# Layer-1 convolution stage: the outputs' inverse scale on GpSimd, hidden tiles transposed one step later

## The reference, cut to what matters

```python
def act_quant(x):
    scale = 127.0 / jnp.clip(jnp.max(jnp.abs(x), axis=-1, keepdims=True), 1e-05)
    return jnp.clip(jnp.round(x * scale), -128, 127) / scale

h = bit_linear(x, w1)                       # layernormed x, quantised; ternary weights; 256 -> 1024
h = depthwise_conv1d(h.transpose(0, 2, 1), conv_w, conv_b)   # three taps along the tokens
h = jax.nn.silu(h.transpose(0, 2, 1))
x = x + bit_linear(h, w2)                   # h quantised by its own maximum per token; 1024 -> 256
```

## Time and profile before

| what | value |
|---|---|
| median of three runs | 3378.53 us |
| the profiled execution's own time | 3373.19 us |
| its span | 3371.5 us |
| busy over the span: TensorE, VectorE, ScalarE, GpSimd | 92%, 73%, 52%, 39% |
| 3079.24 to 3318.11 us: busy of 238.87 us, TensorE | 205.34 us |
| the same, VectorE | 223.69 us |
| the same, ScalarE | 222.33 us |
| the same, GpSimd | 202.39 us |

### The profile page before, as it was taken

One profiled execution on the slowest core, in us unless ns is written; L12 is line 12 of the kernel. 1 busy time (PEld: TensorE's weight loads), 2 busy tenths in 40 slices (PEclk: granted clock), 3 DMA queues, 4 the chain that ended last, 5 costly groups with the idle time before them and its releaser, 6 DMA issues. The chain is left out here.

```text
span 3371.5 us, 63871 instructions
## 1 busy us (share of the span) xinstructions
PE 3090.4 (92%) x23118; PEld 2677.0 (79%) x23118; DVE 2453.9 (73%) x5435; ACT 1760.1 (52%) x4520; POOL 1303.3 (39%) x1199
## 2 busy tenths in 40 slices
PE   6999999999999999999999899999999973168887
PEld 5888888888888888888888788888888861046665
DVE  6666666666666666666666787878787849889998
ACT  5565656565656565656564323232323325169997
POOL 2333333333333333333332333343434320058886
PEclk9999999999999999999999999999999985589999
DMA  5000000000000000000001112121212133011111
GB/s 160 5 8 5 8 5 8 5 7 5 7 5 8 5 8 5 8 5 8 5 5 57 58 42 73 42 74 42 73 42 73 42 76 66 0 33 38 45 38 38
DMA packets 108790, 103.92 MB, mean 31 GB/s; under 512 B 26584, under 2 KB 87744, under 8 KB 108480
## 3 DMA queue, kind: packets, MB, share of 16 engines
q1 hardware_dynamic: 108480, 99.84, 10.3%
HBM read 86.61 MB, written 13.21 MB: 30 GB/s over the span
## 5 line engine op out<-in xcount | busy, mean ns | idle before, releaser
L794 POOL TENSOR_TENSOR attention_prob<-attention_prob,attention_inv_sums 128x1024 f32<-128x1024 f32 x256 | 480.0, 1896 | 399.0 <-DVE attention_inv_sums L652 399.0
L504 ACT ACTIVATE attention_prob<-attention_turns,attention_neg_max 128x256 f32<-128x256 f32 x1024 | 468.5, 482 | 175.2 <-DVE attention_neg_max L643 175.2
L1371 POOL TENSOR_TENSOR experts_hidden_lo<-experts_weighed,experts_hidden_hi 128x512 fp32r<-128x512 f32 x192 | 255.1, 1329 | 530.4 <-ACT experts_hidden_hi L1124 530.3
L659 DVE COPY attention_probT<-attention_turns 128x512 f32<-128x512 f32 x512 | 328.8, 684 | 163.0 <-PE attention_turns L380 162.9
L346 PE MATMUL attention_turns<-kv_hi,wkv 128*128 128x512 f32 x1024 | 374.1, 406 | 0.0
L643 DVE TENSOR_REDUCE attention_neg_max<-attention_turns 128x2 f32<-128x512 f32 x512 | 317.8, 683 | 45.2 <-PE attention_turns L370 44.3
L1124 ACT ACTIVATE experts_hidden_hi<-experts_weighed 128x512 fp32r<-128x512 f32 x192 | 121.4, 632 | 406.5 <-DVE experts_weighed L1261 406.5
L314 PE MATMUL attention_turns<-wkv,kv_hi 128*128 128x512 f32 x1024 | 329.3, 403 | 2.1 <-DVE kv_lo L677 2.1
L495 ACT COPY attention_v<-attention_turns 128x512 f32<-128x512 f32 x256 | 150.1, 586 | 310.1 <-PE attention_turns L314 310.1
L380 PEld LDWEIGHTS attention_turns<-ident,attention_prob 128*128 128x128 f32 x2048 | 240.2, 141 | 36.5 <-POOL attention_prob L794 3.1
L380 PE MATMUL attention_turns<-ident,attention_prob 128*128 128x128 f32 x2048 | 266.2, 273 | 2.5 <-POOL attention_prob L794 2.5
(11 more groups left out here) (296 smaller groups left out, 8938.2 us busy)
## 6 DMA issues: line engine op xcount, KB each, us to landing
experts_spread<-shares SPq DMA_DIRECT2D x256, 128.0 KB, 3.0
attention_ctx<-in_ctx SPq DMA_DIRECT2D x32, 256.0 KB, 2.7
experts_far_ctxT<-in_ctxT SPq DMA_DIRECT2D x32, 256.0 KB, 3.5
weights_ctx<-in_ctx SPq DMA_DIRECT2D x16, 512.0 KB, 3.9
out<-conv_x_out SPq DMA_DIRECT2D x15, 512.0 KB, 2.8
x_all<-in_x SPq DMA_DIRECT2D x7, 1024.0 KB, 9.7
first_x<-norms SPq DMA_DIRECT2D x16, 256.0 KB, 3.2
dist<-experts_far SPq DMA_DIRECT2D x16, 256.0 KB, 2.4
```

Source lines behind the costliest of these rows:

```text
L504: made = act.activation(prob[n % 2][:, h, :], bank_of("s", 2 * n + e)[:, m * 256:(m + 1) * 256], ACT.Exp, bias=neg_max[:, n % 2, 2 * e + m ...
L659: dve.tensor_copy(probT[n % 2][:, 2 * g:2 * g + 2].rearrange("p h t c -> p (h t c)"), bank_of("t", 2 * n + g)[:, :]).then_inc(p_copied, 1)
L794: pool.tensor_tensor(prob[n % 2][:, :, :], prob[n % 2][:, :, :], inv[:, n % 2, :].unsqueeze(2).broadcast_to([P, QH, 2 * TOK]), ALU.mult).t ...
L1371: pool.tensor_tensor(hid_lo[n % 3][:, :], weighed[n % 2], hid_hi[n % 3][:, :].bitcast(F32), ALU.subtract).then_inc(hid_split, 1)
```

## The change

Two edits, and their semaphores. First, the product that makes `inv2` leaves `hidden_scale` on VectorE and becomes `unscale` on GpSimd, at m5 of the next group in place of m4, with a semaphore `inv2_made` that `weigh_out`, `finish_last` and the next `hidden_scale` wait for. Second, TensorE transposes tile n-5 in step n where it transposed tile n-4. The semaphore `ones_set` is merged into `terms_made`, whose count 2 takes its place.

```diff
 # TensorE, loop
-                if tile(n - 4):
-                    turn_hidden(n - 4)
+                if tile(n - 5):
+                    turn_hidden(n - 5)
 # ScalarE, weigh_out
+                act.wait_ge(inv2_made, g + 1)
 # VectorE, hidden_scale
+                if g:
+                    dve.wait_ge(inv2_made, g)
 ...
                 dve.reciprocal(q2[:, :], amax2[:, :]).then_inc(q2_made, 1)
-                if g >= 3:
-                    dve.wait_ge(out_weighed, 2 * (g - 2))
-                dve_step(dve, dve.tensor_scalar(inv2[g % 3][:, :], amax2[:, :], w_mean[:, 1:2], None, ALU.mult))
 # VectorE, finish_last
+                    dve.wait_ge(inv2_made, NG)
 # SyncE
-            sp.wait_ge(ones_set, 1)
+            sp.wait_ge(terms_made, 2)
 # GpSimd
-                pool.memset(term_rows[:, :, :], 1.0).then_inc(ones_set, 1)
+                pool.memset(term_rows[:, :, :], 1.0).then_inc(terms_made, 1)
 ...
+            def unscale(g):
+                pool.wait_ge(q2_made, g + 1)
+                if g >= 3:
+                    pool.wait_ge(out_weighed, 2 * (g - 2))
+                pool.tensor_scalar(inv2[g % 3][:, :], amax2[:, :], w_mean[:, 1:2], None, ALU.mult).then_inc(inv2_made, 1)
 ...
+                if m == 5 and live(g - 1):
+                    unscale(g - 1)
```

More of the change, by code:

```diff
@@ L1757, in conv_ffn @@
         ramp_made, bounds_made, bounds_copied = st.sems("ramp_made", "bounds_made", "bounds_copied")
-        terms_made, terms_stored, ones_set, terms_loaded, shape_made, form_made, outside_made = st.sems(
-            "terms_made", "terms_stored", "ones_set", "terms_loaded", "shape_made", "form_made", "outside_made")
+        terms_made, terms_stored, terms_loaded, shape_made, form_made, outside_made = st.sems(
+            "terms_made", "terms_stored", "terms_loaded", "shape_made", "form_made", "outside_made")
         path_made, expanded, x_added = st.sems("path_made", "expanded", "x_added")
@@ L1766, in conv_ffn @@
         h_turned, h_maxed, q2_made, q2_turned = st.sems("hidden_turned", "hidden_maxed", "q2_made", "q2_turned")
-        h_scaled = st.sem("h_scaled")
+        h_scaled, inv2_made = st.sems("h_scaled", "inv2_made")
         pool_rounded, act_rounded, dve_rounded = st.sems("pool_rounded", "act_rounded", "dve_rounded")
@@ L2173, in hidden_scale @@
             def hidden_scale(g):
-                s = g % 2
                 dve.wait_ge(h_maxed, TILES * (g + 1))
+                if g:
+                    dve.wait_ge(inv2_made, g)
                 dve_step(dve, dve.tensor_reduce(amax2[:, :], hmax[:, :, :], AX.X, ALU.max))
```

## The result

The median of the kernel after is 3471.38 us (four runs, 3469.26 to 3478.98) against 3377.93 us of the kernel before on the same chip (3369.82 to 3378.57). The ratio is 1.0286, its 95% interval 1.0273 to 1.0298: slower by 93.5 us, where 65 had been forecast. The profiled execution took 3470.06 us.

What follows compares the result with a forecast made beforehand. It took nearly full VectorE, and who waits for whom, as the bound. New waits of VectorE summed to 52.4 us, TensorE's clock 13: 3378.5 + 65 = 3444 us, with 3408 to 3466 for 8 in 10.

Steps and rivals of the forecast that it cites:

- The product: L2183 leaves VectorE, saving 1.00 us of the group, own work 22.15 us; on GpSimd 0.3 us at no cost.
- The waits of VectorE: VectorE's waits for the turned tile: 1.23 us at m0, 3.07 at m2, 0.15 at m4, 0.70 at m5.
- three things stand ahead of it there: TensorE's step n: hidden at m0, turn(g+1, 0) at m2, turn(g+1, 1) at m5 hold the tile; 1.23, 3.07, 0.70 us.
- 27.30: VectorE's steady group after the change, in us: own work 22.15 plus the new waits, 3.38 more than 23.92.
- 52.4: Sum in us without the clock: eleven steady groups 37.2, two before them 9.4, group 1 4.3, the last 1.5.
- the clock, 13 us: TensorE's half clock after idle time: 0 to 2.8 us a group, taken as 1.1, 13 us over twelve groups.
- two idle stretches: TensorE idle some 3.5 us before hidden at m0, and from about 6.5 to 9.06 at m2, lowering its clock.
- The rule of the Trainium skill: TensorE's gate is closed by default, opened by activity; both idle times paid every group, sum near its upper end.
- (a): Rival: VectorE relieved, turned tiles ready in time, nothing comes back; 1.3 us less a group, 3360 us; chance 0.07.
- (b): Rival: only m0 and m5 bind, as GpSimd works through faster; group 24.4 us, total 3388 us; chance 0.06.
- (c): Rival: only m2 and m5 bind; 26.0 us a group, about +35, total 3413 us; chance 0.07.
- (d): Rival: GpSimd collision moves to hidden_scale's other tensor_scalar, up to 0.9 us a group, 12 us; 3456 us; chance 0.08.

Runs made afterwards that it cites:

- product: The kernel before with the first edit alone: product on GpSimd, tiles turned in n-4's place as before; 3363.35 us, ratio 0.9967.
- warm16: The changed kernel plus unread transposes in TensorE's four longest idle times, 16 of them ahead of hidden at m0, clock at 1.00; 3441.34 us, ratio 1.0199.
- m0_first: The changed kernel with the turned tile put ahead of hidden at m0; 3433.47 us, ratio 1.0174.
- m2_last: The changed kernel with the input's transposes, turn(g+1, 0), moved behind the turned tile and outputs at m2; 3461.20 us, ratio 1.0260.
- best: The changed kernel with the turned tile first in every step, spread_scale behind it at m6, turn(g+1, 0) last at m2; 3370.11 us, ratio 0.9986.
- three: The changed kernel with the tile's turn first at m0, turn(g+1, 0) last at m2, spread_scale behind the turn at m6; 3421.74 us, ratio 1.0140.
- turn: The kernel before with the second edit alone: tile turned a step later, product left on VectorE; 3499.88 us, ratio 1.0373.
- best_warm: The changed kernel reordered with every holder behind the tile, plus unread transposes, 12 at m0 and 8 ahead of turn(g+1, 1); 3360.47 us, ratio 0.9958.

## Why the prediction was right on the side and short on the size

**The product.** Right: VectorE's own work, taken as 22.15 us, was 22.04 in product, and 0.31 us on GpSimd cost nothing, as taken. The run gained 12 us where 9 had been expected of it.

**The waits of VectorE.** Counted 1.23, 3.07, 0.15 and 0.70 at m0, m2, m4 and m5; at full clock (warm16) they are 1.15, 3.02, 0.23 and 0.62. Adding distances along the holder's path, from start to start, priced those at m0, m2 and m5 within 0.1 us; the one at m4 was the middle of a range. At the real clock of the kernel after they are 1.87, 2.54, 0.37 and 0.68. m0_first and m2_last show that the two holders named are the cause of m0 and m2. That of m5 is seen in the timeline alone: no run removes it on its own, best removes it with the others.

**The step that failed: "in TensorE's program three things stand ahead of it there, each behind a wait of its own".** There are four. I listed what stands ahead of the tile within its own step, and `spread_scale` stands at the end of the step before. Its wait for `scale_tile` costs 1.61 us a group at m6 at full clock. Against it VectorE's own work is 21.72 us, 0.43 less than counted, of which product explains 0.11. The other 0.32 are all at m6, which without its wait takes 3.97 us in product and 3.65 in warm16. They are in the two tensor_scalars of `find_scale` (product, then warm16):

```profile
3222.81 0.22 DVE L2142 TENSOR_SCALAR conv_x_inv<-conv_x_absmax 128x4 f32<-128x4 f32 x1
3223.06 0.52 DVE L2145 TENSOR_SCALAR conv_x_unit<-conv_x_inv,weights_mean 128x4 f32<-128x4 f32 x1
...
3218.97 0.17 DVE L2156 TENSOR_SCALAR conv_x_inv<-conv_x_absmax 128x4 f32<-128x4 f32 x1
3219.18 0.23 DVE L2159 TENSOR_SCALAR conv_x_unit<-conv_x_inv,weights_mean 128x4 f32<-128x4 f32 x1
```

In product GpSimd is at work beside them, and each ends as an operation of GpSimd does (its `add_side` at 3223.00, its cast at 3223.56); in warm16 VectorE comes to them 1.6 us later and GpSimd is idle. So the wait at m6 gave a fifth of its price back. The group at full clock is 28.35 us, not 27.30: 11 us over eleven groups, and the total says the same, 63.4 against 52.4 (against the kernel before on warm16's own chip it is 65.7).

**The term that was mis-sized: the clock, 13 us.** It is 30 us (3471.38 less 3441.34). I had bounded it at 0 to 2.8 us a group from two idle stretches, and taken 1.1. It is 2.3 (30.63 less 28.35), but not where I looked for it. The waits of m0 to m2 grow by 0.92 us together, that of m6 by 0.97, a place that the forecast had no wait at: in the kernel after it is 1.6 us in four groups and 3.0 to 3.2 in seven; a row of m6 at 3295.28 us has a tag of 3.03, where that at 3231.65 has 1.52. Of my two idle times the one at m0 was followed by half clock in all eleven steady groups, the one at m2 in three. The rule of the Trainium skill that I had weighed, "TensorE: Matmul & The Clock Gate", Part 1, pointed to the upper end; the size came out near it, but the way there (both idle times paid in every group) the trace does not bear out. A count in that step was off by one as well: in the kernel before, half clock followed the wait at m7 in ten of the twelve groups, not in nine. 11 + 17 us, from the two errors, are the 28 us that the forecast lacks.

**The rivals.** (a) falls: product shows what the group would be with nothing coming back, 23.0 us, and no kernel with the tile late and all its holders in place is under 28.3. (b) falls by the 3.02 us at m2 in warm16, (c) by the 1.15 at m0. (d) is seen, but small in the kernel after: L2179 took 0.37 to 0.53 us in three of its eleven steady groups and 0.95 once outside them, its median is 0.17. In m2_last, three and best it comes in many groups at the 0.9 us that (d) had named. All sixteen in the kernel after (instances, ns min/median/max, first and last start):

```profile
L2179 DVE TENSOR_SCALAR conv_h_absmax<-conv_h_absmax x16: 170/172/947, 3014.4 to 3449.3; 128x4 f32<-128x4 f32 x16
```

## What to carry to other kernels

When an operation is moved later on an engine that works in order, list everything that now stands between it and its old place, the end of the step before included, and price each wait by start-to-start distances along the chain that releases it. A wait that had cost nothing because its engine ran a step ahead becomes the price of every group once the step of slack is spent. Where such waits leave TensorE idle, look for low clock behind every one of them, take its price nearer to the upper bound than to the middle (here 2.3 of 2.8 us), and measure the edits with the clock held, or the clock hides what each is worth.

## What the runs showed of the hardware

**The clock makes a pattern of its own.** In m2_last seven of eleven groups are 30.7 to 30.8 us long, in best every second one is 25.0 and the others 22.6. In best TensorE stands idle 1.45 and 0.48 us at the change of groups, and then is granted half clock while it is busy without a pause. But the idle time does not decide it alone: it is the same 1.45 and 0.47 us at the start of the short groups, where the clock stays at 1.00. The rows are TensorE's at the start of a short group and of the long one behind it, then 3 us of the long one's window:

```profile
3208.81 0.63 PE L1907 MATMUL conv_hidden_turned<-ident,conv_act_h 128*128 128x128 f32 x4 [1.45 <-DVE conv_h_absmax_part L2175]
...
3231.43 0.63 PE L1907 MATMUL conv_hidden_turned<-ident,conv_act_h 128*128 128x128 f32 x4 [1.45 <-DVE conv_h_absmax_part L2175]
3232.53 0.50 PE L1897 MATMUL conv_h_ps<-conv_xT_hi,weights_w_ternary 128*128 128x512 f32 x1 [0.48 <-DVE conv_xT_lo L2162]
```

```profile
3233.00:3236.00 3.00, 3.00 (x13) 0.50 0.00 0
```

So it is open why long and short alternate. The kernel before has it too: the same 2.27 to 2.29 us of idle time at m7 are followed by half clock in most groups and by full clock in two. What the runs show is that unread transposes in the gaps end it: 3471 to 3441 us in the kernel after, and the groups of best all at 22.64 us. In product they change nothing that the times can tell apart (3363.35 and 3361.77); its trace has the group at 23.02 us without them and at 22.78 with them.

**A tiny tensor_scalar can cost 1.06 us.** In best, L2183 of 128x4 starts 0.16 us after GpSimd's L2309 of 128x508 and ends with it, at 3247.83 and 3247.82, where the same operation otherwise takes 0.17 us. The Trainium skill, "SBUF — State Buffer", section "Who interferes with whom", says that a tensor_scalar of VectorE in its two-port mode and an instruction of GpSimd exclude each other for the length of the one that came first. The trace agrees, with 0.94 us here, up to 1.06 at the other L2183, the product on VectorE in turn, and the pair of `find_scale` above. In these kernels the same operation on the same tile is short or long by the phase of the two engines; best_warm, where VectorE comes to m4 on time, has it at 0.17 us in every steady group.
